# A two-layer convolution block: the offset convolution moved from column halves to 32 by 32 tiles of the array, in four phases

## What is computed

```python
def _L0_conv_ref(x, w_off, b_off, w_dcn, b_dcn):
    off = (sigmoid(conv2d(x, w_off, b_off, 1)) - 0.5) * 2.0     # 3x3, 32 -> 64 channels
    # off[:, 0] and off[:, 1]: a shift of less than one pixel in x and y, per channel and pixel
    sampled = bilinear(x, ix - off_x, iy - off_y)               # reflected at the borders
    return conv2d(sampled, w_dcn, b_dcn, 1)                     # 3x3, 32 -> 32 channels

def _L1_conv_ref(x, w1, b1, w2, b2):
    hdn = relu(x.mean(axis=(2, 3)) @ w1 + b1)
    kernels = (hdn @ w2 + b2).reshape(b, 32, 3, 3)              # one 3x3 kernel per image and channel
    return depthwise_conv2d(x, kernels)

x = x + _L0_conv_ref(_gn(x), ...)     # _gn: group norm over pairs of channels
x = x + _L1_conv_ref(_gn(x), ...)
```

## Time and profile before

| | |
|---|---|
| median of three runs | 1492.13 us |
| the profiled execution | 1493.54 us, its span 1491.7 us |
| granted clock of TensorE, mean | 0.992 |
| instructions | 30369 |
| busy PE / DVE / ACT / POOL | 96% / 84% / 77% / 29% of the span |
| DMA | 308.8 MB, mean 207 GB/s |

### The profile page before, as it was taken

The page is one execution under the profiler, slowest core; times in us unless marked ns, Lnnn a source line. Parts: engine busy times, 40 slices in busy tenths (PEclk is TensorE's granted clock), DMA queues, the critical chain, the costliest instruction groups (busy, mean ns, idle before and its releaser), DMA issues.

```text
span 1491.7 us, 30369 instructions
## 1 busy us (share of the span) xinstructions
PE 1436.3 (96%) x12300; PEld 617.9 (41%) x12300; DVE 1257.4 (84%) x884; ACT 1152.9 (77%) x1970; POOL 437.1 (29%) x474
## 2 busy tenths in 40 slices
PE   5898798999999999999999999999999999999978
PEld 2333343444444444444444444444444444444433
DVE  4999999988888898889888988888888889888900
ACT  6789687986888778887888877888688877766643
POOL 5000734225050432306141151412505043230120
PEclk9999999999999999999999999999999999999999
DMA  8576587977888788886979778897888877767558
GB/s 270 159 191 170 146 215 182 242 197 204 236 224 217 198 213 228 228 216 179 244 206 255 189 206 230 223 233 194 205 236 224 217 199 180 198 179 201 140 145 260
DMA packets 226907, 308.77 MB, mean 207 GB/s; under 512 B 17216, under 2 KB 169152, under 8 KB 226768
## 3 DMA queue, kind: packets, MB, share of 16 engines
q1 hardware_dynamic: 211360, 266.68, 61.2%
q0 software_dynamic: 15408, 40.15, 17.3%
HBM read 190.35 MB, written 38.14 MB: 153 GB/s over the span
## 4 chain that ended last, share of the span: by engine, by line
PE 89%; DVE 4%; DMA 2%; issue 2%; ACT 2%; POOL 1%; SPq 0%; DVEq 0%; ACTq 0%; POOLq 0%
PE z L402 46%; PE dc L442 24%; PE dw L475 14%; PE z L475 3%; DMA yr<-in_planes 1%; DVE nb L840 1%; DVE nb L838 1%; DMA yh<-yr 1%; DVE nb L818 1%; DVE nb L835 0%; PE dc L451 0%; ACT nb L635 0%; DVE nb L844 0%; DVE nb L842 0%; PE z L494 0%
## 5 line engine op out<-in xcount | busy, mean ns | idle before, releaser
L402 PE MATMUL z<-xv,wos 128*64 128x384 f32 x4608 | 766.1, 488 | 10.7 <-issue 7.6
L402 PEld LDWEIGHTS z<-xv,wos 128*64 128x64 f32 x4608 | 330.7, 137 | 429.8 <-issue 428.6
L442 PE MATMUL dc<-sr,wds 128*32 128x384 f32 x2304 | 396.4, 489 | 13.4 <-issue 9.5
L442 PE MATMUL dc<-sh,wds 128*32 128x384 f32 x2304 | 396.4, 489 | 0.0
L1017 POOL DMA_DIRECT2D yr<-in_xr x96 | 86.2, 898 | 767.1 <-ACT yr L669 767.1
L818 DVE COPY_PREDICATED nb<-mu,xv 128x2280 f32<-128x2280 uint16 x96 | 269.2, 2804 | 36.9 <-ACT mu L621 36.5
L442 PEld LDWEIGHTS dc<-sr,wds 128*32 128x32 f32 x2304 | 133.5, 108 | 237.2 <-issue 237.1
L475 PE MATMUL dw<-yh,wy 128*64 128x388 f32 x616 | 229.7, 494 | 0.0
L475 PE MATMUL dw<-yr,wy 128*64 128x388 f32 x616 | 229.7, 494 | 0.0
L635 ACT ACTIVATE nb<-xv 128x2292 f32<-128x2292 f32 x96 | 202.9, 2113 | 28.8 <-DVE sr L851 20.6
L614 ACT ACTIVATE du<-z,ob 128x768 f32<-128x768 f32 x96 | 86.4, 900 | 128.8 <-PE z L402 128.2
(11 more groups left out here) (130 smaller groups left out, 1594.6 us busy)
## 6 DMA issues: line engine op xcount, KB each, us to landing
xv<-in_x SPq DMA_DIRECT2D x272, 384.0 KB, 5.6
yr<-in_xr POOLq DMA_DIRECT2D x96, 392.0 KB, 5.0
out<-ot SPq DMA_DIRECT2D x96, 388.0 KB, 3.9
yh<-yr SPq DMA_DIRECT2D x178, 196.0 KB, 3.9
st<-in_planes SPq DMA_DIRECT2D x56, 576.0 KB, 7.5
sh<-sr SPq DMA_DIRECT2D x160, 194.0 KB, 5.1
sh<-sr SPq DMA_DIRECT2D x32, 145.5 KB, 5.7
yr<-in_planes SPq DMA_DIRECT2D x8, 576.0 KB, 10.3
```

The lines of the kernel that those rows point to most:

```text
L402: last = nc.tensor.matmul(acc[m], weights[:, kx, :], view[:, :, kx:kx + W], start=kx == 0, stop=kx == 2)
L442: last = nc.tensor.matmul(dc[m, q, 0:NB * PAIRS], weights[:, kx, q], view[:, :, cols], start=first, stop=final)
```

## The change

The offset convolution is computed in products of 32 rows and 32 columns: one line group of the input, one tap of the nine, one output line. For each output line and bank there are nine such products, without the two zero blocks, so a chunk has 144 calls (288 instructions) in place of 24 (48). tap_plan() spreads them: in phase p the input quarter g works on bank (g + p) % 4, so that the four row groups write four different banks; each phase has 32 calls and the first one 48. Before each phase but the first PE waits for z_turn, which the last product of the phase before it raises. For this plan two lines more of each chunk are needed, above the middle view and below it; xv gets a fifth block per view (xf is its flat view), x_load two small loads (24 KB) more, and POOL two more border rows but one border column operation in place of two.

In PE's loop the two depthwise halves move between phases 0 and 1 and phases 1 and 2. Off_mm is raised by two after the last phase, so both L614 of ACT are released together, and phase 0 of the next chunk waits for both to be read. In ACT's loop evacuate moves behind the first finish, the second finish before the offsets, and x_sums behind it. The weights wo and wos have 576 columns per partition in place of 384.

```diff
@@ -27,6 +28,7 @@
 EPS = 1e-5
 CNT = HW // G
 STILES = 8
+SLOTS = NB + 1
...
@@ -65,7 +67,7 @@
 
 
 def x_dmas(n):
-    return 3 + (n % CHUNKS in (0, CHUNKS - 1))
+    return 5
 
 
 def s_dmas(n):
...
@@ -102,6 +104,41 @@
 
     at = first // 2 if first % 2 else PAIRS + first // 2
     return slice(at, at + PAIRS)
+
+def tap_plan():
+
+    at = {ABOVE: 0, MID: SLOTS, BELOW: 2 * SLOTS}
+    plan = {}
+    for row in range(G):
+        source = {(g, g + view - row): at[view]
+                  for g in range(G) for view in (ABOVE, MID, BELOW) if 0 <= g + view - row <= 2}
+        if row == 0:
+            source[G - 1, 0] = at[MID] - 1
+        if row == G - 1:
+            source[0, 2] = at[MID] + 1
+        taps = sorted(itertools.product(range(3), range(3)), key=lambda t: sum(ky == t[0] for _, ky in source))
+        for bank in range(4):
+            room = [2 + (g == bank) for g in range(G)]
+            used = [[] for _ in range(G)]
+
+            def place(i):
+                if i == len(taps):
+                    return True
+                ky, kx = taps[i]
+                for g in sorted(range(G), key=lambda g: sum(a == g for a, _ in source)):
+                    if (g, ky) in source and len(used[g]) < room[g]:
+                        used[g].append((source[g, ky], ky, kx))
+                        if place(i + 1):
+                            return True
+                        used[g].pop()
+                return False
+
+            assert place(0)
+            plan[row, bank] = used
+    return plan
 
 
 def small_order():
...
@@ -126,7 +163,9 @@
         def sem(name):
             return ctx.enter_context(nc.semaphore(name))
 
-        xv = [sb(f"xv{s}", [P, 3, NB, WP]) for s in range(XS)]
+        xs = [sb(f"xv{s}", [P, 3, SLOTS, WP]) for s in range(XS)]
+        xv = [t[:, :, 0:NB, :] for t in xs]
+        xf = [t[:].rearrange("p v k w -> p (v k) w") for t in xs]
         nb = [sb(f"nb{s}", [P, 3, NB, W]) for s in range(2)]
         du = [sb(f"du{s}", [P, NB, W]) for s in range(2)]
         dv = [sb(f"dv{s}", [P, NB, W]) for s in range(2)]
...
@@ -141,11 +180,11 @@
         ot = [sb(f"ot{s}", [P, NB, Q, OW]) for s in range(2)]
         st = [sb(f"st{s}", [P, SW]) for s in range(2)]
         junk = sb("junk", [P, N], BF16)
-        wo = sb("wo", [P, 2, 3, 2 * C])
-        wo_sum = sb("wo_sum", [P, 2, 2 * C])
+        wo = sb("wo", [P, 2, 9, C])
+        wo_sum = sb("wo_sum", [P, 2, 3, C])
         wd_sum = sb("wd_sum", [P, Q, C])
         mr = [sb(f"mr{s}", [P, 1]) for s in range(2)]
-        wos = [sb(f"wos{s}", [P, 2, 3, 2 * C]) for s in range(2)]
+        wos = [sb(f"wos{s}", [P, 2, 9, C]) for s in range(2)]
         wd = sb("wd", [P, 3, Q, C])
         wds = [sb(f"wds{s}", [P, 3, Q, C]) for s in range(2)]
         wdc = sb("wdc", [P, 3, Q, C])
...
@@ -297,6 +337,12 @@
                         k1 = NB - 1
                     sp.dma_start(v[:, view, k0:k1, 1:W + 1],
                                  blocks_of(b, line + P * k0, k1 - k0)).then_inc(done, 16)
+                if j > 0:
+                    sp.dma_start(xf[n % XS][P - C:P, SLOTS - 1, 1:W + 1],
+                                 lines[b, P * k - C:P * k, :]).then_inc(done, 16)
+                if j < CHUNKS - 1:
+                    sp.dma_start(xf[n % XS][0:C, SLOTS + NB, 1:W + 1],
+                                 lines[b, P * (k + NB):P * (k + NB) + C, :]).then_inc(done, 16)
 
             def st_load(b, i):
                 wait(sp, st_used, b * STILES + i - 1)
...
@@ -396,26 +442,33 @@
             halves = (slice(0, 2 * C), slice(2 * C, P))
             quarters = [slice(C * g, C * g + C) for g in range(G)]
 
-            def conv(acc, weights, whole, moved):
-                for kx in range(3):
-                    for m, view in zip(halves, (whole, moved)):
-                        last = nc.tensor.matmul(acc[m], weights[:, kx, :], view[:, :, kx:kx + W],
-                                                start=kx == 0, stop=kx == 2)
-                return last
-
-            def offsets(n, i):
+            plan = tap_plan()
+
+            def offsets(n, phase):
                 b, j = divmod(n, CHUNKS)
-                v = xv[n % XS]
-                if i == 0:
+                v = xf[n % XS]
+                if phase == 0:
                     pe.wait_ge(x_in[n % XS], ring(n, XS, x_dmas))
                     pe.wait_ge(pads, pads_set(n))
                     if j == 0:
                         pe.wait_ge(wo_ok, b + 1)
-                wait(pe, z_read, 2 * (n - 1) + i + 1)
-                for h in range(2):
-                    k = slice(HALF * h, HALF * h + HALF)
-                    last = conv(z[:, i, h, 0:HALF * W], wos[b % 2][:, i], v[:, ABOVE, k, :], v[:, BELOW, k, :])
-                last.then_inc(off_mm, 1)
+                    wait(pe, z_read, 2 * n)
+                else:
+                    pe.wait_ge(z_turn, 3 * n + phase)
+                for t in range(3 if phase == 0 else 2):
+                    for g, rows in enumerate(quarters):
+                        bank = (g + phase) % 4
+                        i, h = divmod(bank, 2)
+                        for m in range(G):
+                            at, ky, kx = plan[m, bank][g][t]
+                            last = nc.tensor.matmul(z[quarters[m], i, h, 0:HALF * W],
+                                                    wos[b % 2][rows, i, 3 * ky + kx],
+                                                    v[rows, at + HALF * h:at + HALF * h + HALF, kx:kx + W],
+                                                    start=phase == 0 and t == 0, stop=phase == 3 and t == 1)
+                if phase < 3:
+                    last.then_inc(z_turn, 1)
+                else:
+                    last.then_inc(off_mm, 2)
 
             def deform(n, q):
                 b, j = divmod(n, CHUNKS)
...
@@ -498,9 +551,10 @@
                 small_turn("ob", b)
                 mean = mr[b % 2][:]
                 for i in range(2):
-                    for g, m in enumerate(quarters):
-                        half = slice(C * (g % 2), C * (g % 2) + C)
-                        nc.tensor.matmul(sm[m, C_OB + i:C_OB + i + 1], wo_sum[:, i, half], mean, start=True, stop=True)
+                    for m in quarters:
+                        for ky in range(3):
+                            nc.tensor.matmul(sm[m, C_OB + i:C_OB + i + 1], wo_sum[0:C, i, ky], mean[0:C],
+                                             start=ky == 0, stop=ky == 2)
                 for q in range(Q):
                     for m in quarters:
                         last = nc.tensor.matmul(sm[m, C_DB + q:C_DB + q + 1], wd_sum[:, q], mean,
...
@@ -556,12 +610,14 @@
                 c, d = i - DW_STEP, i - DCN_STEP
                 if b and o == 7:
                     y_bias(b - 1)
+                offsets(i, 0)
                 if c >= 0:
                     depthwise(c, 0)
-                offsets(i, 0)
                 offsets(i, 1)
                 if c >= 0:
                     depthwise(c, 1)
+                offsets(i, 2)
+                offsets(i, 3)
                 if d >= 0:
                     deform(d, 0)
                 if b and o == 5:
...
@@ -740,12 +796,6 @@
             for i in range(TOTAL):
                 b, o = divmod(i, CHUNKS)
                 c, e = i - DW_STEP, i - DCN_STEP - 1
-                if e >= 0:
-                    evacuate(e)
-                if b + 1 < B and 1 < o <= STILES + 1:
-                    x_sums(b + 1, o - 2)
-                    if o == STILES + 1:
-                        x_totals(b + 1)
                 if b and o == 4:
                     read("ym", b - 1, mvy[:], sm[:, C_YM:C_YM + 2])
                 if b and o == 5:
...
@@ -762,14 +812,20 @@
                     act.wait_ge(small_rd, SMALL["wb", b - 1] + 1)
                 if c >= 0:
                     finish(c, 0)
+                if e >= 0:
+                    evacuate(e)
+                if c >= 0:
+                    finish(c, 1)
+                if b + 1 < B and 1 < o <= STILES + 1:
+                    x_sums(b + 1, o - 2)
+                    if o == STILES + 1:
+                        x_totals(b + 1)
                 offset(i, 0)
                 side(i, 0)
                 size(i, 0)
                 offset(i, 1)
                 side(i, 1)
                 size(i, 1)
-                if c >= 0:
-                    finish(c, 1)
                 if e >= 0:
                     y_square(e)
                 if b and o == 3:
...
@@ -926,16 +982,17 @@
                         pool.wait_ge(x_step, X_STEPS * (b + 2))
                     elif j > 0:
                         pool.wait_ge(wy_ok, b)
-                    q, view, k = (slice(0, C), ABOVE, 0) if j == 0 else (slice(P - C, P), BELOW, NB - 1)
+                    top, end = slice(0, C), slice(P - C, P)
+                    q, view, k = (top, ABOVE, 0) if j == 0 else (end, BELOW, NB - 1)
```

(13 more changed lines are left out.)

19 lines of the change are left out of this document (11 added, 8 removed).

## The result

The changed kernel takes **1722.42 us** (median of 4 runs, 1711.58 to 1727.57), the kernel before 1492.15 beside it: ratio **1.153** (95% interval 1.148 to 1.159). I had forecast 1486, at most 1562. The profiled execution took 1721.74 us, its span is 1719.9 and the mean granted clock 0.968 (before 0.992).

What follows compares the result with a forecast made beforehand. DVE was taken to bound the first 19 chunks, PE the other 77. From 1493.5 us, -40 (ordinary chunks), +19 (y sums), +12 (scaled weights) and +3 (small things) gave 1487.5, against the median 1486; range 1430 to 1562.

Steps and rivals of the forecast that it cites:

- the late results: Two stalls of PE once per image, for the y sums and the scaled weights: +19 us and +12 us.
- Saved 1.93 us ... I take 18 [rounds]: Offset convolution on PE: 18 rounds of 0.3225 us with 16 tiles side by side, in place of 24, per chunk.
- Filling 16 tiles ... 0.10 in each of four phases.: Start of each offset phase on PE: the last of 16 tiles starts later, +0.40 us per chunk.
- Issue is no limit: 10 ns each.: PE's offset products: tiny products start every 10 ns with weight load, while 16 tiles need one per 20 ns.
- Four more [changes of shape] at 0.15 = +0.60.: PE's changes of tile shape: six per chunk in place of two, +0.60 us per chunk.
- Turn +0.40.: Between offset phases off2 and off3 on PE: waiting until the earlier phase has written its banks, +0.40 us per chunk.
- The y sums ... +19 us.: Chunk 3 of an image: PE idles 3.2 us for ACT's late y totals, six times, +19 us.
- The scaled weights ... +2.0 us.: First offsets of the next image: PE waits for POOL's late weights, +2.0 us, six times, +12 us.
- The first 19 chunks ... first chunk +2.: Program start: DVE bounds the first 19 chunks, so change there is worth little; first chunk's later ACT read, +2 us.
- A set of 16 runs at two thirds of full pace: Rival on the offset rounds: 2.96 us more per chunk, 1736 us; chance 0.12 together with half running at a time.
- the row groups' disturbance: Rival: each round of 16 tiles takes longer than 0.3225 us; 1736 or 2007 us, chance 0.12 together.
- Handing over is dear: Rival: changes of shape at 0.3 us, filling 0.2 per phase, chunk 15.0 us; 1562 or 1524 us, chance 0.20.

Runs made afterwards that it cites:

- e1: The changed kernel with each row group adding all nine products into its own bank, one piece without turns between phases: 1915.7 us, ratio 1.283.
- e2: The changed kernel with offset products in 32 x 128 tiles, 36 calls per chunk in place of 144, same four phases: 1527.4 us, ratio 1.023.
- e8: The changed kernel with offset products in 32 x 64 tiles, 72 calls per chunk in place of 144, same four phases: 1520.9 us, ratio 1.019.
- e9: The changed kernel with the two inner loops of offsets() exchanged, so successive calls go to the four row groups: 1706.8 us, ratio 1.144.
- e6: The changed kernel with 192 columns per offset product in place of 384: 1647.0 us, ratio 1.104.
- e5: The kernel before with 120 one-column calls added per chunk on PE, without row tiles: 1773.0 us, ratio 1.188.
- e10: The kernel before with its products unchanged, but PE's and ACT's steps in the order of the change: 1600.4 us, ratio 1.072.
- e4: The changed kernel with a quarter of the loads of x, of the residual and of the stores: 1626.1 us, ratio 1.089.
- e11: The kernel before in the order of the change, but ACT evacuates first and sums y early in chunk 3: 1569.1 us, ratio 1.051.

## Why the prediction was wrong, step by step

The profiled execution took 234 us more than the 1487.5 of my sum. 100 of them are the quiet chunk (+0.79 for -0.53, 76 times), 59 the holes at fetches, 31 the low clock, 30 the chunks ahead of chunk 19, and 8 the end; the late results cost 4 less than their terms, and 10 are spread. The quiet chunk alone turned the sign.

- **"Saved 1.93 us ... I take 18 [rounds]" of 0.3225 us: the step that failed, in the size of a round.** The 18 rounds are right, the pace is not. 16 tiles need 0.83 us for 16 calls (e1), 0.41 per round, and with 18 of them the saving is 0.3 us in place of 1.93. I had the two bounds "all side by side" and "in turns" and took the first by rows with at most four tiles. e2 and e8 show that the reason (row groups do not hinder each other) held.
- **"Filling 16 tiles ... 0.10 in each of four phases."** This is the same failure. The bound I wrote beside it, "if the look-ahead holds only half of the tiles' calls", was the right mechanism with a wrong place: the look-ahead runs out at every set, not only at a phase's start. In the changed kernel the first 16 tiles start 6.7 ns apart, the 17th call at 0.67 us, when the first tile's second product has had its 0.32, and the next ones from 0.86 us on, 16.7 ns apart. That fits a queue that holds 16 calls (64 instructions) ahead and takes about 0.2 us to bring a fresh call to a free tile: 16 tiles use all of it in one set (33 weight loads, then none for 0.22 us), eight tiles have a second call waiting (e8), the order of the calls is nothing (e9), the cost is per set and not per column (e6). The queue itself was not looked into; its size and the 0.2 us are inferred from these. The Trainium skill (TensorE: Matmul & The Clock Gate, Part 1, Architectural detail) gives TensorE a queue depth of 64; by that figure (an estimate) 16 calls, each two weight loads and two products, fill it, and the starts above agree.
- **"Issue is no limit: 10 ns each."** True of the rate (8.5 ns in e5), false of the supply. I counted issue and forgot that 30369 instructions (of all engines) become 77130, and each has to be fetched through DMA engines that are busy 85% of the time. No row of before showed such a hole. 59 us of holes, and the clock that falls with some of them. The Trainium skill (Runtime: NRT & Kernel Launch, Instruction fetch mechanics) has the instructions come in blocks of 16 KiB, 256 each, and calls the cost of crossing a block mostly hidden. The place of the holes agrees with the blocks; "hidden" held for the kernel before (no such hole in some 77 fetches between chunks 19 and 95) and not here.
- **"Four more [changes of shape] at 0.15 = +0.60."** Measured 0.09 to 0.10 over a round each (gaps of 0.41 to 0.42 from the last start to the next shape's first), in e2 and e8 as well. A change of row tiling costs no more than one of column tiling. The 0.15 was too much for the kernel before already: from 712.90 to 713.32 in the earlier trace rows is 0.42, 0.10 over a round. The pieces have 0.35 us over 20 rounds (1.40 + 4.04 + 1.36 less 6.45), not 0.32, and the rest of it lies inside them.
- **"Turn +0.40."** Off2 to off3 is 0.54 from start to start, 0.22 over a round; 0.29 in e8.
- The Trainium skill (TensorEngine Tiling (Array Packing), Tiling Modes) says that changing the mode drains the engine. The gaps of 0.41 us are shorter than the 0.49 us that a product is modelled to take, so these runs show no full drain.
- **"The y sums ... +19 us."** The mechanism is right: 2.8 us of idling per image for 3.2. In the faster chunks of e10 it is 5.4 on the mean. What I left out is what goes with such a hole: the clock stands at half for a stretch. That price was in no term, and in e10 it is more than half of the holes themselves (39 us for 68).
- **"The scaled weights ... +2.0 us."** The right queue (residual, normalisation, borders, weights on POOL behind the evacuation), the wrong item and size. The borders of chunk 11 are due 14.5 us before the scaled weights and were done 10.7 us after the residual's start in e10; I had looked at chunk 12 only. It is 1.5 us in four of six images in the change, where the added border row took 3.3 us, and 5 to 7 in e10. PE did wait for the scaled weights in e1, 16.0 us in five times. The weights, with a DVE that idles more, took 1.74 us for 576 columns where the earlier trace rows has 3.81 for 384.
- **"The first 19 chunks ... first chunk +2."** Wrong, +32. I had looked at ACT's first L614 alone. 17 of the 32 come ahead of chunk 3, where PE waits 10.5 us for the reads of z (before 3.1), with the clock that goes with it; the forecast took the reads as hidden behind the deformable product, and there is none yet. They stay with light DMA (e4, 15.9). With light DMA the other half goes; what share of it the fetches have was not tried.
- **The rivals.** "A set of 16 runs at two thirds of full pace" gave 1736, near the result, but that is luck: it had 225 us of slower rounds, where the quiet chunks missed the forecast by 100 and the holes, the clock and the start brought the rest. The pace was 0.78 of full, and the row groups' disturbance that it named does not exist. The sentence beside it, on the Trainium skill (TensorE: Matmul & The Clock Gate, Part 3: Packing small matmuls), took its 10.6 times for 16 tiles as a steady pace of two thirds; measured in e1 are 0.645 / 0.83 of 16, some 12.4. "Handing over is dear" named the changes of shape and the filling; the filling was dear. My 0.12 for both cases together was too little for the one step that no row covered.

## What to carry to other kernels

Count what a packing does to the number of instructions before counting the rounds it saves: 32 by 32 tiles in fp32 take two products per call and 16 calls per set, and the lost look-ahead, the fetches and the clock took back all of a saving of a quarter (24 rounds to 18). Eight tiles at a time kept full pace and had no holes at fetches. And when an order is changed, follow the queue behind the moved step to its last item on every engine: here one evacuation, 5 to 8 us later in its chunk, held border rows at the end of POOL's queue, and in e10 and e11 the holes cost about half of themselves again in clock.

## What the runs showed of the hardware that I had not expected

- 16 tiles of two-product calls run at 0.83 us per 16 calls in a long piece, 8 and 4 tiles at 0.323 us per round; the order of row and column groups does not matter to 0.01 us (e1, e2, e8, e9).
- Products on 32 rows run side by side as well as those on 128, and a change between 32-row and 128-row tiles costs 0.10 us.
- Instruction fetches became visible with 71192 products and weight loads in the span in place of 24600: up to 3.2 us of standstill at one place in every 256 instructions of PE, 59 us in all with the DMA engines busy for 70% of the span, 9 us with a quarter of the loads of x, of the residual and of the stores, none with 43544 (e8), 152 us when the products are half as long.
- The granted clock went to half around all twelve holes of 3.3 to 7.0 us between chunks 19 and 95 of e10, and around four of the six waits of 2.4 to 2.8 us for the y sums in the change (not at 1091 and 1303 us); a hole of 1.9 us idle at 919.5 us had it too. Two late results per image cost 39 us in clock over the run (e10), one of them 24 (e11).
